# Attention over normalised feature maps: a prologue in units of 512 columns, f moved by DMA, and weighing begun ahead of the second chunk's scores

## The chip, the cores and the metric

The kernel runs on one core of a Trainium2 chip. The metric is the device time in microseconds (us) of one execution. The kernel before takes 1973.11 us, the median of 3 runs from 1971.37 to 1973.39.

Five engines work side by side, each through its own list of instructions in order, and wait for one another by semaphores: PE (TensorE, matrix products), DVE (VectorE), ACT (ScalarE), POOL (GpSimd) and SP (SyncE), which here issues all DMAs. An instruction that waits holds up everything behind it on its engine.

## The reference

For each of 4 images of 256 channels and 4096 pixels, what is computed is

```
n      = groupnorm(x)                 # 32 groups of 8 channels, over channels and pixels
f, g   = Wq n, Wk n                   # 64 x 4096 each
h      = Wv n                         # 256 x 4096
beta   = softmax(f^T g, axis=1)       # 4096 x 4096: over the rows, for each column m
out    = x + gamma * (h beta) + n     # 256 x 4096
```

## The kernel before

An image is a batch (b). Its 4096 output columns are done in 16 chunks of 256, so there are K = 64 chunks; k counts them through all images, and j is the chunk's number in its image. The 4096 rows of a chunk's scores are done in G = 8 groups of 4 x 128 rows. A step n = 8k + g is one group of one chunk. Every product is made of float16 parts, high and low (F1 holds f with high and low part in its two halves of partitions, G1 and GL hold g's high and low parts, V both parts of h).

The main loop goes over the 512 steps. At step n PE weighs: `weigh` multiplies the exponentials PH and PL of the step with V (24 matmuls of 256 or 257 columns). At each even step it first makes the scores of two groups (`scores(q)`, 16 matmuls into the two halves of S) of the chunk two ahead, q = n + 16. ACT copies each of these tiles to SBUF (`store`) and makes exponentials (`exps`, twice), DVE takes running maxima (`maximum`), turns and reduces them once a chunk (`turn_maxima`, `quadrant_maxima`, `column_maxima`, `spread_maxima`) and subtracts them (`subtract`), and POOL makes PL (`low_weights`). In the middle of a chunk PE sums maxima over partitions (`share_maxima`).

A finished chunk is scaled and turned by DVE (`turn_blocks`), regrouped by 16 small DMAs (`regroup`, 32 partitions each), added to the residual by POOL (`add_attention`) and stored (`store` on SP). SP's list for chunk k is: regroup(k-1), store(k-1), the residual's input for k+1, an input piece where one is due, and then the doubling of g.

Before the first step stands the prologue: image 0 is loaded in four pieces of 1024 columns, measured, normalised in place by DVE, split into XH (ACT) and XL (DVE for the first 128 channels, POOL for the others). PE waits for both parts of a piece, then projects f and g (`project_fg`, 8 units of 512 columns, in three banks of O); ACT and DVE split the result into F1, G1, GL by two instructions each over 64 partitions. Then come the scores of chunks 0 and 1 and 16 projections of h (`project_v`), and only then the first subtraction, exponential and weighing.

Units alternate which half of the partitions holds f (`halves`). scores needs g on both halves of the partitions, so SP copies g over (`double_g`). For the next image, the units of f and g are projected in chunk j = 13 (units 0 to 6, one a step) and the first step of j = 14 (unit 7), those of h in j = 15 and j = 0. The scores of the next image begin at the first step of j = 14.

There, the pair made at step g (even) reads f of units g and g+1. The lines before, by which each step can be followed, are L214 to L288 (SP), L303 to L349 (POOL), L436 to L506 (PE), L547 to L585 (ACT) and L767 to L868 (DVE).

Of the kernel before, what the change touches and what calls it, by code (L numbers as in the profile page):

```python
# [5 lines left out]
def groupnorm_attention(nc, x, wqT, wkT, wvT, gamma, out):  # L6
# [51 lines left out]
    NV = 2 * G  # L58
    assert len(FG_AT) == NFG and len(V_AT) + len(V_LATE) == NV
# [4 lines left out]
    with ExitStack() as ctx:  # L64
# [62 lines left out]
        gd2 = MB[:, M + 128:M + 128 + 32].rearrange("p (a b) -> p a b", a=NG)  # L127

        w_in = sem("w_in")
        x0_in = [sem(f"x0_in{i}") for i in range(NPC)]  # L130
# [11 lines left out]
        res_coefs = sem("res_coefs")  # L142
        xn_ready = sem("xn_ready")
# [4 lines left out]
        fg_done = sem("fg_done")  # L148
        g_in = [sem(f"g_in{i}") for i in range(NFG)]
# [35 lines left out]

        def halves(u):

            top, bottom = slice(0, CQ), slice(CQ, P)
            return (bottom, top) if u % 2 else (top, bottom)
# [25 lines left out]
        def _(sp):  # L215
            for q in range(NPC):
                sp.dma_start(x0[:, :, piece(q)], xv[0, :, :, piece(q)]).then_inc(x0_in[q], 16)
# [30 lines left out]

            def double_g(u):

                f, g = halves(u)
                n = slice(u % NFG * FGW, (u % NFG + 1) * FGW)
                sp.wait_ge(fg_done, u + 1)
                sp.dma_start(GG[f, :, n], GG[g, :, n]).then_inc(g_in[u % NFG], 16)

            residual_input(0)
            for u in range(NFG):
                double_g(u)
            for k in range(K):
                b, j = divmod(k, CPB)  # L260
                if k > 0:
                    regroup(k - 1)
                    store(k - 1)
# [3 lines left out]
                if b + 1 < BATCH:  # L267
                    p = j - STAT_FIRST + 1
                    if 0 <= p < NPC:
                        if p > 0:  # L270
                            sp.wait_ge(xin_read, b * NPC + p)
                        elif b > 0:
                            sp.wait_ge(xl_ready[1], NPC * (b + 1))
                            sp.wait_ge(xl_ready[0], NPC * (b + 1))
                        load(b + 1, p)
                    p = j - NORM_FIRST + 1
                    if j == STAT_FIRST + NPC - 1:
                        sp.wait_ge(xin_read, (b + 1) * NPC)
                        load(b + 1, 0)
                    elif 0 < p < NPC:  # L280
                        sp.wait_ge(xl_ready[1], NPC * (b + 1) + p)
# [9 lines left out]
        def _(pool):  # L291
# [11 lines left out]
            for q in range(NPC):  # L303
                pool.wait_ge(xh_ready, 2 * q + 2)
                pool.tensor_tensor(XL[:, 1, piece(q)], x0[:, 1, piece(q)], XH[:, 1, piece(q)],
                                   ALU.subtract).then_inc(xl_ready[1], 1)
# [24 lines left out]
            def low_input(b, p):  # L331
                for h in range(H):
                    pool.wait_ge(xh_ready, 2 * (NPC * b + p) + h + 1)
                    pool.tensor_tensor(XL[:, h, piece(p)], xin[:, h, :], XH[:, h, piece(p)],
                                       ALU.subtract).then_inc(xl_ready[h], 1)
# [16 lines left out]
        def _(pe):  # L352
            mm = nc.tensor.matmul

            def project_fg(u, o):

                b, i = divmod(u, NFG)
                for h in range(H):
                    pe.wait_ge(xl_ready[h], b * NPC + i // 2 + 1)
                n = slice(i * FGW, (i + 1) * FGW)  # L360
                w = slice(i % 2 * CQ, i % 2 * CQ + P)
                for h in range(H):
                    mm(o, wqkh[:, h, w], XH[:, h, n], start=h == 0, stop=False)
                    mm(o, wqkl[:, h, w], XH[:, h, n], start=False, stop=False)
                    m = mm(o, wqkh[:, h, w], XL[:, h, n], start=False, stop=h == H - 1)
# [72 lines left out]
            for i in range(NFG):  # L438
                if i >= OB:
                    pe.wait_ge(fg_done, i - OB + 1)  # L440
                project_fg(i, O[:, i % OB, :])
                if i % 2 == 1 and i >= 3:
                    pe.wait_ge(fg_done, i - 1)
                    if i == 3:
                        pe.wait_ge(g_in[0], 16)
                    scores((i // 2 - 1) * 2)
            pe.wait_ge(fg_done, NFG)
            scores(G - 2)
            for u in range(NV):
                if u >= 2:  # L450
                    pe.wait_ge(v_done, u - 1)
                project_v(u, O[:, u % 2, :])
                if u % 2 == 1 and u < G:
                    scores(G + u - 1)
                if u == 8:
                    share_maxima(0, O[:, 2, :])
# [14 lines left out]
            for n in range(K * G):  # L471
                k, g = divmod(n, G)
                b, j = divmod(k, CPB)
                if g % 2 == 0 and k + 2 < K:
                    nb, i = divmod(k + 2, CPB)
                    if i == 0:
                        pe.wait_ge(fg_done, nb * NFG + g + 2)
                    if g == 0 and i % 2 == 0:
                        pe.wait_ge(g_in[i // 2], 16 * (nb + 1))
                    if g == 4:  # L480
                        pe.wait_ge(mxc_ready, k + 2)
                    scores(n + 2 * G)
                pe.wait_ge(pl_ready, n + 1)
                if g == 0:
                    if k == 0:
                        pe.wait_ge(mxc_ready, 1)
# [10 lines left out]
                if g == 3 and k + 1 < K:  # L497
                    read = min(n + 2 * G + 1, K * G)
# [10 lines left out]
        def _(act):  # L509
# [16 lines left out]
            def round_fg(u, o):  # L526
                f, g = halves(u)
                n = slice(u % NFG * FGW, (u % NFG + 1) * FGW)
# [21 lines left out]
            for q in range(NPC):  # L550
                for h in range(H):
                    act.wait_ge(xn_ready, H * q + h + 1)
                    nc.scalar.copy(XH[:, h, piece(q)], x0[:, h, piece(q)]).then_inc(xh_ready, 1)
            for i in range(NFG):
                round_fg(i, O[:, i % OB, :])
                if i % 2 == 1 and i >= 3:
                    if i == 3:
                        for h in range(H):
                            act.wait_ge(xl_ready[h], NPC)
                    store(i - 3)  # L560
                    store(i - 2)
            store(G - 2)
            store(G - 1)
            for u in range(NV):
                round_v(u, O[:, u % 2, :])
                if u % 2 == 1 and u < G:
                    store(G + u - 1)
                    store(G + u)
            for s in range(EXP_LEAD):
                exps(s)  # L570

            for n in range(K * G):
# [4 lines left out]
                if g % 2 == 0 and k + 2 < K:  # L577
                    store(n + 2 * G)
                    store(n + 2 * G + 1)
                extra(k, g, MID)  # L580
                extra(k, g, END)
                if g in (4, 6) and b + 1 < BATCH and NORM_FIRST <= j < NORM_FIRST + NPC:
                    p, h = j - NORM_FIRST, g // 2 - 2
                    act.wait_ge(xn_ready, H * ((b + 1) * NPC + p) + h + 1)
# [3 lines left out]
        def _(dve):  # L588
# [128 lines left out]
            def low_fg(u, o):  # L717
                f, g = halves(u)
                n = slice(u % NFG * FGW, (u % NFG + 1) * FGW)
# [54 lines left out]
            for q in range(NPC):  # L774
                dve.wait_ge(x0_in[q], 16)
                for a in range(2 * q, 2 * q + 2):
                    for h in range(H):
                        last = ve.bn_stats(stats[:, h, a, :], x0[:, h, a * 512:(a + 1) * 512])
# [7 lines left out]
            for q in range(NPC + 1):  # L786
                if q < NPC:
                    for h in range(H):
                        normalise(x0[:, h, piece(q)], h).then_inc(xn_ready, 1)
                if q > 0:  # L790
                    dve.wait_ge(xh_ready, 2 * q)
                    ve.tensor_tensor(XL[:, 0, piece(q - 1)], x0[:, 0, piece(q - 1)], XH[:, 0, piece(q - 1)],
                                     ALU.subtract).then_inc(xl_ready[0], 1)
                if q == 0:
                    dve.wait_ge(w_hi, 1)
                    ve.tensor_tensor(wqkl[:, :, :], wqk[:, :, :], wqkh[:, :, :], ALU.subtract).then_inc(w_split, 1)
                    ve.tensor_tensor(wvl[:, :, :], wv[:, :, :], wvh[:, :, :], ALU.subtract).then_inc(w_split, 1)
            for i in range(NFG):
                low_fg(i, O[:, i % OB, :])
                if i % 2 == 1 and i >= 3:  # L800
                    maximum(i - 2)
                    maximum(i - 3)
            maximum(G - 1)
            maximum(G - 2)
            turn_maxima(0)
            for u in range(NV):
                low_v(u, O[:, u % 2, :])
                if u % 2 == 1 and u < G:
                    maximum(G + u)
                    maximum(G + u - 1)  # L810
                if u == 5:
                    quadrant_maxima(0)
                if u == G - 1:
                    turn_maxima(1)
                if u == 10:
                    column_maxima(0, O[:, 2, :])
                    spread_maxima(0)
# [77 lines left out]
```

## Time and profile before

| | |
|---|---|
| median of 3 runs | 1973.11 us |
| the profiled execution | 1974.76 us, its span 1973.0 us |
| mean granted TensorE clock | 0.993 of full speed |
| PE busy | 96% of the span |
| DVE, ACT, POOL busy | 82%, 81%, 66% |
| first matmul | 29.82 us |
| first weighing matmul | 104.88 us |

The engine table says how long each engine was busy. The timeline has an instruction (or several alike, merged, with their count) in each row: its start, how long it took, engine, line, operation, and in brackets how long the engine had been idle and what released it. The landing of a DMA is counted from its issue on SP. PEclk is the clock granted to TensorE as a share of full speed; 1.00 is its 2.4 GHz level and 0.50 its 1.2 GHz level.

### The profile page before, as it was taken

To read this page: it belongs to the slowest core of one execution; us is meant where nothing else is said; L and a number is where in the kernel's file an instruction comes from. 1 tells how busy PE (TensorE), PEld (TensorE's weight loads), DVE (VectorE), ACT (ScalarE), POOL (GpSimd) and SP (SyncE) were. 2 spreads that over 40 slices of the span, in tenths; PEclk is the share of its full clock that TensorE was granted. 3 is DMA by queue.
4 is the path that set the end of the run, shared out by engine and by line. 5 is a ranking of instruction groups with operands and counts; after the bars stand their busy time and mean duration, and the time that the engine had idled before them with its cause. 6 is when DMAs were issued, how large, how long until landed. Compare 5 with 4: busy or idle time off the path is not lost. (4 is left out here: it accounts for less than half of the span.)

```text
span 1973.0 us, 44069 instructions
## 1 busy us (share of the span) xinstructions
PE 1899.5 (96%) x17476; PEld 1565.3 (79%) x17476; DVE 1617.9 (82%) x1961; ACT 1590.3 (81%) x1699; POOL 1299.8 (66%) x746
## 2 busy tenths in 40 slices
PE   2889999999999999999999999999999999999999
PEld 1578888887788888888777888888878788888887
DVE  7778899888777899897876889998787778878784
ACT  3588888988777888898876888889887688888885
POOL 2066767876546766887554677688655476676776
PEclk9899999999999999999999999999999999999999
DMA  3012212211112121221110221121111011111111
GB/s 110 12 31 73 75 23 54 73 31 23 49 23 69 46 75 30 61 67 23 47 25 17 74 73 54 24 75 53 30 41 32 18 33 33 23 32 31 32 32 35
DMA packets 193629, 86.97 MB, mean 44 GB/s; under 512 B 149137, under 2 KB 186257, under 8 KB 193425
## 3 DMA queue, kind: packets, MB, share of 16 engines
q1 hardware_dynamic: 193424, 84.16, 16.2%
q8 instruction: 139, 2.28, 0.5%
q14 instruction: 66, 0.53, 0.1%
HBM read 46.60 MB, written 16.78 MB: 32 GB/s over the span
## 5 line engine op out<-in xcount | busy, mean ns | idle before, releaser
L310 POOL TENSOR_TENSOR PL<-SC,PH 128x1024 f16<-128x1024 f32 x512 | 1091.3, 2137 | 636.3 <-ACT SC L524 634.3
L416 PE MATMUL O<-V,PH 128*128 128x257 f16 x4096 | 1119.9, 273 | 9.4 <-POOL PL L310 5.2
L418 PE MATMUL O<-V,PL 128*128 128x257 f16 x4096 | 1119.8, 273 | 0.0
L417 PE MATMUL O<-V,PH 128*128 128x256 f16 x4096 | 1118.1, 273 | 0.0
L523 ACT ACTIVATE PH<-SC 128x1024 f16<-128x1024 f32 x512 | 540.6, 1056 | 134.3 <-PE O L418 121.6
L714 DVE TENSOR_TENSOR SC<-SC,MB 128x1024 f32<-128x1024 f32 x512 | 614.9, 1211 | 0.4
L517 ACT ACTIVATE SC<-S 128x1024 f32<-128x1024 f32 x512 | 502.5, 1012 | 124.5 <-issue 106.2
L674 DVE TENSOR_TENSOR XM<-S,XM 128x1024 f32<-128x1024 f32 x384 | 468.1, 1219 | 130.6 <-PE S L404 129.2
L524 ACT ACTIVATE SC<-SC 128x1024 f32<-128x1024 f32 x512 | 534.8, 1044 | 0.0
L416 PEld LDWEIGHTS O<-V,PH 128*128 128x128 f16 x4096 | 406.6, 99 | 59.2 <-DVE OSB L750 6.0
L417 PEld LDWEIGHTS O<-V,PH 128*128 128x128 f16 x4096 | 401.3, 98 | 50.7
L418 PEld LDWEIGHTS O<-V,PL 128*128 128x128 f16 x4096 | 401.4, 98 | 50.3
L398 PE MATMUL S<-GG,F 128*128 128x256 f16 x1024 | 155.5, 275 | 7.4 <-DVE XM L674 3.8
L401 PE MATMUL S<-GG,F 64*128 64x256 f16 x2048 | 158.0, 274 | 0.0
L404 PE MATMUL S<-GG,F 128*128 128x256 f16 x1024 | 157.8, 277 | 0.0
L669 DVE TENSOR_TENSOR XM<-S,SC 128x1024 f32<-128x1024 f32 x64 | 78.3, 1224 | 92.7 <-ACT SC L517 92.7
L404 PEld LDWEIGHTS S<-GG,F 128*128 128x128 f16 x1024 | 79.7, 98 | 61.1 <-issue 54.8
L401 PEld LDWEIGHTS S<-GG,F 64*128 64x128 f16 x2048 | 79.5, 95 | 60.9 <-issue 54.5
L398 PEld LDWEIGHTS S<-GG,F 128*128 128x128 f16 x1024 | 100.1, 98 | 24.7 <-issue 9.2
L728 DVE TENSOR_TENSOR V<-O,V 128x512 f16<-128x512 f32 x64 | 43.6, 688 | 62.0 <-ACT V L537 61.6
L537 ACT CAST V<-O 128x512 f16<-128x512 f32 x64 | 37.1, 587 | 66.6 <-PE O L377 66.6
L329 POOL TENSOR_TENSOR RES<-RES,ATT 128x512 f32<-128x512 f32 x63 | 80.6, 1280 | 0.9 <-DMA ATT<-OT 0.9
(84 smaller groups left out, 1138.5 us busy)
## 6 DMA issues: line engine op xcount, KB each, us to landing
xin<-x SPq DMA_DIRECT2D x24, 1024.0 KB, 5.9
xres<-x SPq DMA_DIRECT2D x64, 256.0 KB, 2.9
out<-RES SPq DMA_DIRECT2D x64, 256.0 KB, 2.2
ATT<-OT SPq DMA_DIRECT2D x1008, 16.0 KB, 1.9
SC<-x SPq DMA_DIRECT2D x4, 1024.0 KB, 8.7
GG<-GG SPq DMA_DIRECT2D x32, 128.0 KB, 2.4
SC<-wvT SPq DMA_DIRECT2D x1, 256.0 KB, 9.4
SC<-wqT SPq DMA_DIRECT2D x2, 64.0 KB, 10.5
```

The source lines that it names most:

```text
L310: pool.tensor_tensor(PL[:, s % RING, :], sc(s), PH[:, s % RING, :], ALU.subtract).then_inc(pl_ready, 1)
L398: mm(to(a, i), F1[:, rows(a, i)], G1[:, cols], start=True, stop=False)
L401: mm(to(a, i), F1[half, rows(a, i)], GL[half, cols], start=i % 2 == 1, stop=i % 2 == 0)
L404: m = mm(to(a, i), F1[:, rows(a, i)], G1[:, cols], start=False, stop=True)
L416: mm(o[:, 0:C + 1], PH[:, n % RING, cols], vh, start=t == 0, stop=False)
L417: mm(o[:, 0:C], PH[:, n % RING, cols], vl, start=False, stop=False)
L418: w = mm(o[:, 0:C + 1], PL[:, n % RING, cols], vh, start=False, stop=t == T - 1)
L517: nc.scalar.activation(sc(q), S[:, q % 2, :], ACT.Copy).then_inc(s_stored, 1)
L523: nc.scalar.activation(PH[:, s % RING, :], sc(s), ACT.Exp, bias=SHIFT)
L524: nc.scalar.activation(sc(s), sc(s), ACT.Exp, bias=SHIFT).then_inc(exp_done, 1)
L674: ve.tensor_tensor(XM[:, :], scores, XM[:, :], ALU.max).then_inc(s_maxed, 1)
L714: ve.tensor_tensor(tile, tile, MB[:, 0:M].unsqueeze(1).to_broadcast([P, GT, M]), ALU.subtract).then_inc(sub_ready, 1)
```

## The change

- The input of image 0 comes in eight pieces of 512 columns. Per unit, ACT makes XH straight from x with scale and bias, DVE normalises the first 128 channels into a spare bank of S (`x0n`), POOL the others into `xin` (`x1n`), and each subtracts XH to get its XL. The low parts of the weights move from DVE to POOL.
- PE begins a unit's products with XH before its XL is there, and projects h of a unit right behind its f and g, in five banks (three of O, two of S).
- The result of `project_fg` is rounded whole: one ACT instruction writes G1 and one DVE instruction GL, over all 128 partitions. f is then in G1 and GL, and two DMAs (`move_f`) take its parts to F1. `double_g` overwrites f's place with g and so waits until both have landed (semaphores `f_in`). scores waits for `f_in` of its two units where it had waited for `fg_done`. This holds for all four images.
- `SCORES_AT` says at which step which pair of score tiles is made. The prologue makes the pairs 0 to 6 (chunk 0) and 8 and 10; pairs 12 and 14 come in steps 1 and 2, chunk 2's in steps 4 to 7, one a step, and from step 8 on the order is the old one.

```diff
+    SCORES_AT = {1: 12, 2: 14, 4: 16, 5: 18, 6: 20, 7: 22}
+    SCORES_AT.update({n: n + 2 * G for n in range(G, (K - 2) * G, 2)})
...
+            def move_f(u):
+
+                f, g = halves(u)
+                sp.wait_ge(fg_done, u + 1)
+                sp.dma_start(F1[f, unit(u)], G1[f, unit(u)]).then_inc(f_in[u % NFG], 16)
+                sp.dma_start(F1[g, unit(u)], GL[f, unit(u)]).then_inc(f_in[u % NFG], 16)
+
             def double_g(u):
 
                 f, g = halves(u)
-                n = slice(u % NFG * FGW, (u % NFG + 1) * FGW)
-                sp.wait_ge(fg_done, u + 1)
-                sp.dma_start(GG[f, :, n], GG[g, :, n]).then_inc(g_in[u % NFG], 16)
+                sp.wait_ge(f_in[u % NFG], 32 * (u // NFG + 1))
+                sp.dma_start(GG[f, :, unit(u)], GG[g, :, unit(u)]).then_inc(g_in[u % NFG], 16)
...
                 if k > 0:
                     regroup(k - 1)
+                    if j == FG_FIRST + 1 and b + 1 < BATCH:
+                        move_f((b + 2) * NFG - 1)
+                        double_g((b + 2) * NFG - 1)
                     store(k - 1)
...
-                    for place, i in FG_AT.items():
-                        if place[0] == j:
-                            double_g((b + 1) * NFG + i)
+                    if j == FG_FIRST:
+                        for u in range((b + 1) * NFG, (b + 2) * NFG - 1):
+                            move_f(u)
+                            double_g(u)
...
             def project_fg(u, o):
...
                 for h in range(H):
-                    pe.wait_ge(xl_ready[h], b * NPC + i // 2 + 1)
...
+                    if b == 0:
+                        pe.wait_ge(xl_ready[h], i + 1)
+                    m = mm(o, wqkh[:, h, w], XL[:, h, unit(i)], start=False, stop=h == H - 1)
...
+            for u in range(NFG):
+                if u >= 3:
+                    pe.wait_ge(v_done, u - 2)
+                project_fg(u, first_bank(2 * u))
+                if u >= 2:
+                    pe.wait_ge(fg_done, u - 1)
+                project_v(u, first_bank(2 * u + 1))
...
+            for i in range(G // 2):
+                pe.wait_ge(f_in[2 * i], 32)
+                pe.wait_ge(f_in[2 * i + 1], 32)
+                if i == 0:
+                    pe.wait_ge(g_in[0], 16)
+                scores(2 * i)
+                later_v(NFG + 1 + i)
+            later_v(NFG + 5)
+            scores(G)
+            later_v(NFG + 6)
+            share_maxima(0, shared0)
+            later_v(NFG + 7)
+            scores(G + 2)
...
             def round_fg(u, o):
...
-                nc.scalar.copy(F1[f, n], o[f, :])
-                nc.scalar.copy(G1[g, n], o[g, :]).then_inc(fg_hi, 1)
+                nc.scalar.copy(G1[:, unit(u)], o).then_inc(fg_hi, 1)
...
             def low_fg(u, o):
...
-                ve.tensor_tensor(F1[g, n], o[f, :], F1[f, n], ALU.subtract)
-                ve.tensor_tensor(GL[g, n], o[g, :], G1[g, n], ALU.subtract).then_inc(fg_done, 1)
+                ve.tensor_tensor(GL[:, unit(u)], o, G1[:, unit(u)], ALU.subtract).then_inc(fg_done, 1)
```

Two places in the order of instructions matter. The first is SP's list in chunk 13, where the next image's units are handed over, and at the start of chunk 14. GG<-GG is a doubling of g, ATT<-OT the regrouping, xres<-x the residual's input. Before:

```order
L234 DMA out<-RES 128x2x256 [waits out_ready]
L226 DMA xres<-x 128x2x256 [waits res_ready]
L254 DMA GG<-GG 64x2x512 [waits fg_done] x7
L243 DMA ATT<-OT 32x4x32 [waits out_ready,osb_turned]
L243 DMA ATT<-OT 32x4x32 x15
L234 DMA out<-RES 128x2x256 [waits out_ready]
L226 DMA xres<-x 128x2x256 [waits res_ready]
L254 DMA GG<-GG 64x2x512 [waits fg_done]
```

Now, from the last of the seven units on (F<-GG are the two pieces of f; the six units before it have the same three rows with their own semaphore):

```order
L270 DMA F<-GG 64x512 [waits fg_done]
L271 DMA F<-GG 64x512
L277 DMA GG<-GG 64x2x512 [waits f_in6]
L260 DMA ATT<-OT 32x4x32 [waits out_ready,osb_turned]
L260 DMA ATT<-OT 32x4x32 x15
L270 DMA F<-GG 64x512 [waits fg_done]
L271 DMA F<-GG 64x512
L277 DMA GG<-GG 64x2x512 [waits f_in7]
L251 DMA out<-RES 128x2x256 [waits out_ready]
```

Seven doublings in a row have become seven groups of three DMAs, each with a wait for the landing of the two before it; unit 7 has moved ahead of the store of chunk 13's result, but still stands behind the regrouping.

The second place is DVE's list around the end of the prologue. V<-O is the low part of h, XM a maximum, SC<-SC,MB a subtraction. Before, between the second chunk's transposition of maxima and the first step:

```order
L680 STREAM_TRANSPOSE MT<-XM 128x1024
L728 TENSOR_TENSOR V<-O,V 128x2x256 x3
L700 TENSOR_REDUCE mxc<-O 128x8
L707 STREAM_TRANSPOSE MB<-mxc 128x256
L728 TENSOR_TENSOR V<-O,V 128x2x256 x5
L714 TENSOR_TENSOR SC<-SC,MB 128x1024 x4
L669 TENSOR_TENSOR XM<-S,SC 128x1024
```

Now, from the first chunk's transposition on:

```order
L745 STREAM_TRANSPOSE MT<-XM 128x1024
L750 TENSOR_REDUCE MB<-MT 128x8
L757 TENSOR_TENSOR mxs<-place,MB 128x32
L790 TENSOR_TENSOR V<-O,V 128x2x256 x2
L765 TENSOR_REDUCE mxc<-MB 128x8
L772 STREAM_TRANSPOSE MB<-mxc 128x256
L779 TENSOR_TENSOR SC<-SC,MB 128x1024
L734 TENSOR_TENSOR XM<-S,SC 128x1024
```

The first subtraction now stands ahead of the second chunk's first maximum, where before it stood behind all eight tiles of that chunk and all of h.

## Rows read from the trace of the kernel before

**Rows 1.** The page, engine table: busy us, share of the span, instructions.

```profile
PE 1899.5 (96%) x17476; PEld 1565.3 (79%) x17476; DVE 1617.9 (82%) x1961; ACT 1590.3 (81%) x1699; POOL 1299.8 (66%) x746
```

**Rows 2.** Timeline, DVE, start: start us, us, instruction [idle before <-releaser].

```profile
14.09 2.47 DVE L778 BATCH_NORM_STATS2 stats<-SC 128x6 f32<-128x512 f32 x4 [0.18 <-DMA SC<-x]
22.50 0.15 DVE L650 SCALAR_TENSOR_TENSOR rbias<-nmean,nrstd 128x2 f32<-128x2 f32 x1
```

**Rows 3.** Groups by form: busy us, mean ns | idle before.

```profile
L319 POOL TENSOR_SCALAR RES<-xres,rscale,rbias 128x256 f32<-128x256 f32 x128 | 70.4, 561 | 0.0
L721 DVE TENSOR_TENSOR F<-O,F 64x512 f16<-64x512 f32 x32 | 22.1, 689 | 24.6 <-ACT GG L531 24.3
L530 ACT CAST F<-O 64x512 f16<-64x512 f32 x32 | 18.5, 580 | 15.2 <-PE O L365 15.2
```

**Rows 4.** Timeline, normalisation of image 0 on DVE and POOL.

```profile
33.88 3.34 DVE L654 TENSOR_SCALAR SC<-SC,nmean,nrstd 128x1024 f32<-128x1024 f32 x2
33.98 2.69 POOL L305 TENSOR_TENSOR XL<-SC,XH 128x1024 f16<-128x1024 f32 x1 [1.70 <-ACT XH L553]
```

**Rows 5.** Timeline, ACT, two projections of h in a row.

```profile
91.06 0.59 ACT L537 CAST V<-O 128x512 f16<-128x512 f32 x1 [2.71 <-PE O L377]
92.37 0.59 ACT L537 CAST V<-O 128x512 f16<-128x512 f32 x1 [0.72 <-PE O L377]
```

**Rows 6.** Timeline, PE and DVE, a pair of score tiles in the prologue.

```profile
78.27 0.61 PE L398 MATMUL S<-GG,F 128*128 128x256 f16 x4 [0.19 <-DVE XM L674]
...
80.00 2.58 DVE L674 TENSOR_TENSOR XM<-S,XM 128x1024 f32<-128x1024 f32 x2 [0.23 <-PE S L404]
...
82.64 0.61 PE L398 MATMUL S<-GG,F 128*128 128x256 f16 x4
```

**Rows 7.** Timeline, the first weighing, and the scores of step 8.

```profile
100.61 1.06 ACT L523 ACTIVATE PH<-SC 128x1024 f16<-128x1024 f32 x1 [1.88 <-DVE SC L714]
...
102.69 8.40 POOL L310 TENSOR_TENSOR PL<-SC,PH 128x1024 f16<-128x1024 f32 x4 [61.17 <-ACT SC L524]
...
104.88 0.40 PE L416 MATMUL O<-V,PH 128*128 128x257 f16 x1 [5.25 <-POOL PL L310]
...
133.13 0.60 PE L398 MATMUL S<-GG,F 128*128 128x256 f16 x4
```

**Rows 8.** Windows, PE after the wait that ended at 104.88: stretch, its length, PE busy, PEclk, DMA share, GB/s.

```profile
106.00:108.00 2.00, 2.00 (x11) 0.50 0.00 0
```

**Rows 9.** Timeline, SP, the three handovers to the next image.

```profile
495.97 5.24 SPq L254 DMA_DIRECT2D GG<-GG  x7
511.93 10.31 SPq L243 DMA_DIRECT2D ATT<-OT  x16
...
974.59 5.24 SPq L254 DMA_DIRECT2D GG<-GG  x7
...
1453.87 5.22 SPq L254 DMA_DIRECT2D GG<-GG  x7
```

**Rows 10.** Timeline, PE, the same stretches.

```profile
500.42 0.60 PE L398 MATMUL S<-GG,F 128*128 128x256 f16 x4
...
516.73 0.38 PE L425 MATMUL S<-mxs,alike 128*128 128x32 f32 x2 [2.09 <-issue]
...
526.63 0.60 PE L398 MATMUL S<-GG,F 128*128 128x256 f16 x4
...
1005.58 0.60 PE L398 MATMUL S<-GG,F 128*128 128x256 f16 x4
...
1483.28 0.60 PE L398 MATMUL S<-GG,F 128*128 128x256 f16 x4
```

**Rows 11.** One line's DMAs: the doubling of g (L254), then the regrouping (L243).

```profile
L254 SPq DMA_DIRECT2D GG<-GG x32: 590/608/981, 41.0 to 1487.3; - x32
DMA to landing us min/median/max: 2.3/2.4/4.2
...
DMA to landing us min/median/max: 1.8/1.9/3.6
```

More of the change, by code:

```diff
@@ L148, in groupnorm_attention @@
         fg_done = sem("fg_done")
+        f_in = [sem(f"f_in{i}") for i in range(NFG)]
         g_in = [sem(f"g_in{i}") for i in range(NFG)]
@@ L215, in _ @@
         def _(sp):
-            for q in range(NPC):
-                sp.dma_start(x0[:, :, piece(q)], xv[0, :, :, piece(q)]).then_inc(x0_in[q], 16)
+            for u in range(NFG):
+                sp.dma_start(x0[:, :, unit(u)], xv[0, :, :, unit(u)]).then_inc(x0_in[u], 16)
             sp.dma_start(wqk[:, :, 0:CQ], wqT.rearrange("(h p) q -> p h q", p=P)).then_inc(w_in, 16)
@@ L549, in _, with later_v @@
             nc.scalar.copy(wvh[:, :, :], wv[:, :, :]).then_inc(w_hi, 1)
[L550 to L569, printed above, removed]
+            act.wait_ge(res_coefs, 1)
+            for u in range(NFG + 2):
+                if u < NFG:
+                    for h in range(H):
+                        nc.scalar.activation(XH[:, h, unit(u)], x0[:, h, unit(u)], ACT.Identity,
+                                             bias=rbias[:, 0, h:h + 1], scale=nrstd[:, h:h + 1]).then_inc(xh_ready, 1)
+                if u >= 2:
+                    round_fg(u - 2, first_bank(2 * (u - 2)))
+                    round_v(u - 2, first_bank(2 * (u - 2) + 1))
+            def later_v(u):
+                round_v(u, O[:, u % OB, :])
+            later_v(NFG)
+            act.wait_ge(w_split, 2)
+            for i in range(G // 2):
+                store(2 * i)
+                store(2 * i + 1)
+                later_v(NFG + 1 + i)
+            later_v(NFG + 5)
+            for h in range(H):
+                act.wait_ge(xl_ready[h], NFG)
+            store(G)
+            store(G + 1)
+            later_v(NFG + 6)
+            later_v(NFG + 7)
+            exps(0)
+            store(G + 2)
+            store(G + 3)
+            for s in range(1, EXP_LEAD):
                 exps(s)
@@ L576, in _ @@
                     exps(n + EXP_LEAD)
-                if g % 2 == 0 and k + 2 < K:
-                    store(n + 2 * G)
-                    store(n + 2 * G + 1)
+                q = SCORES_AT.get(n)
+                if q is not None:
+                    store(q)
+                    store(q + 1)
                 extra(k, g, MID)
@@ L773, in _ @@
             ve.memset(cv[:, :], 1.0)
[L774 to L778, printed above, removed]
+            for u in range(NFG):
+                dve.wait_ge(x0_in[u], 16)
+                for h in range(H):
+                    last = ve.bn_stats(stats[:, h, u, :], x0[:, h, unit(u)])
             last.then_inc(x0_measured, 1)
@@ L798, in _ @@
[L798 to L804, printed above, removed]
-            turn_maxima(0)
[L806 to L817, printed above, removed]
@@ L818, in _, with first_half @@
-            for s in range(SUB_LEAD):
+            def first_half(u):
+                if u >= 2:
+                    dve.wait_ge(xl_ready[0], u - 1)
+                ve.tensor_scalar(x0n[:, u % 2, :], x0[:, 0, unit(u)], nmean[:, 0:1], nrstd[:, 0:1],
+                                 ALU.subtract, ALU.mult).then_inc(x0n_ready, 1)
+            first_half(0)
+            for u in range(NFG + 2):
+                if u < NFG:
+                    if u + 1 < NFG:
+                        first_half(u + 1)
+                    dve.wait_ge(x0n_ready, u + 1)
+                    dve.wait_ge(xh_ready, H * u + 1)
+                    ve.tensor_tensor(XL[:, 0, unit(u)], x0n[:, u % 2, :], XH[:, 0, unit(u)],
+                                     ALU.subtract).then_inc(xl_ready[0], 1)
+                if u >= 2:
+                    low_fg(u - 2, first_bank(2 * (u - 2)))
+                    low_v(u - 2, first_bank(2 * (u - 2) + 1))
@@ new lines, in later_v @@
+            def later_v(u):
+                low_v(u, O[:, u % OB, :])
+            later_v(NFG)
+            for i in range(G // 2):
+                maximum(2 * i + 1)
+                maximum(2 * i)
+                if i < G // 2 - 1:
+                    later_v(NFG + 1 + i)
+            turn_maxima(0)
+            quadrant_maxima(0)
+            later_v(NFG + 4)
+            later_v(NFG + 5)
+            column_maxima(0, shared0)
+            spread_maxima(0)
+            subtract(0)
+            maximum(G + 1)
@@ L819, in _ @@
+            maximum(G)
+            later_v(NFG + 6)
+            subtract(1)
+            later_v(NFG + 7)
+            maximum(G + 3)
+            maximum(G + 2)
+            for s in range(2, SUB_LEAD):
                 subtract(s)
@@ L826, in _ @@
                     scale_output(k - 1)
-                if g % 2 == 0 and k + 2 < K:
-                    maximum(n + 2 * G + 1)
+                q = SCORES_AT.get(n)
+                if q is not None:
+                    maximum(q + 1)
                 if n + SUB_LEAD < K * G:
                     subtract(n + SUB_LEAD)
-                if g % 2 == 0 and k + 2 < K:
-                    maximum(n + 2 * G)
+                if q is not None:
+                    maximum(q)
+                if n == 2:
+                    turn_maxima(1)
+                    quadrant_maxima(1)
                 if g == 7 and k + 2 < K:
```

123 lines of the change are left out of this document (62 added, 61 removed).

## The prediction

> **What bounds the kernel now.** I read the engine table first: PE is busy for 96% of the span [rows 1]. So time is to be had only where PE stands still or runs at its lower clock. PE's timeline says where that is: it does no weighing before 104.88 [rows 7], and in the main loop it waits little, the longest of it at the three places where one image hands over to the next (2.09 us before a sum of maxima at 516.73, a little more at the other two) [rows 10]. The change touches both places, so I worked each out: the time at which PE begins the scores of step 8, 133.13 before [rows 7], from which on the order is the old one, and the handovers, where f now goes by DMA.
>
> **The prologue: coefficients.** The last four measurements of x wait for the last piece at 14.09 and take 2.47, 0.62 each [rows 2]. With pieces half as large two remain, so the coefficients, ready at 22.65, are ready at 21.4. The bounds are no gain and 1.6.
>
> **The prologue: units.** ACT makes two XH of 512 columns (0.58 each, the time of a copy of 64x512 [rows 3]), so PE starts at about 22.7. A projection of h takes PE 1.31, the distance of two roundings [rows 5]; f and g of a unit have the same number of columns, so a unit takes 2.6. Eight units and the ninth h make 22.2. The first 3 us after a wait run at half the clock (0.50 in 106 to 108 [rows 8]), which costs 1.5. PE is through at 46.3. Is another engine later? DVE has four instructions a unit. At 0.69 [rows 3] they are 2.8, eight units 22.1 from 21.5 on, so it ends beside PE. POOL has two: a tensor_scalar of twice 0.56 [rows 3] and a subtraction of half of 2.1, the time of 128x1024 [rows 7], together 2.2. Beside DVE's in-place normalisation such a subtraction took 2.69 and DVE's pair 3.34 [rows 4]. With these the two are 2.5 to 2.9 a unit. I take 2.4, hidden behind PE; 2.9 would put the scores 2 us later.
>
> On this last point a rule of the Trainium skill bears: "VectorE: DVE Perf Modes", section "Why PSUM operands drop a tier", says that the double-rate mode of fp32 needs both SBUF read ports and isn't to be had with a PSUM operand. DVE's new target is in PSUM, so by the rule its slow-down beside POOL [rows 4] should not come back, and POOL would stay near 2.2 a unit. The trace of before has no such instruction. By either the sum is the same, since 2.2 and 2.5 both hide behind 2.6.
>
> **The prologue: scores.** From the start of a pair to DVE's first maximum are 1.73, the two maxima take 2.58 less an overlap, and the next pair starts behind them [rows 6]. Before, with two projections of h between, the pairs stood 4.37 apart [rows 6]; with one between, PE has 2.9 of work and the chain of 4.2 sets the distance. Four pairs end at 46.3 + 17.2 = 63.5. Then DVE turns, reduces, takes two low parts, spreads and subtracts: the subtraction ends at 69.6. ACT has a store that waits for the next maximum (70.7) and two roundings ahead of the first exponential, so that starts at 72.9. Exponential to POOL is 2.1, POOL to weighing 2.2 [rows 7]: weighing begins at 77.1, 27.8 earlier.
>
> **The ramp.** Most of that is given back. Steps 0 to 7 now hold six pairs of tiles instead of four. A weighing has twice the columns of a projection of h, 2.62 [rows 5], a pair takes PE 1.52 (the 1.73 of [rows 6] less the way to DVE). The 8 weighings are 21.0, six pairs 9.1, the sum of maxima 0.4. To this come 3.1 for two starts at half the clock (step 0, and behind the wait in step 3), and waits: 1.9 for the maxima ahead of pair 14, 2.5 for the maxima of chunk 1, which DVE turns only after pair 14, and 1.1 ahead of most pairs from step 5 to step 8, because a pair and a weighing (4.1) are shorter than the way of a pair through DVE (1.73, then a maximum, a subtraction and a maximum, 1.15 each: 5.2): 4.7 in all. The sum is 42.7, so step 8 starts at 119.8 instead of 133.13: **13.3 less**. Bounds: 5 less, if POOL needs 2.9 a unit and each of the chains in the ramp is a third longer; 18 less, if the waits of the ramp but one fall away.
>
> **The handovers.** Here the change adds waits to SP's list. Before, SP issued the seven doublings in one go, from T = 495.97, 974.59 and 1453.87, in 5.2 us, and the regrouping came 16 us after T and took 10.31 [rows 9]. Now each unit is two moves and one doubling that waits for the second move's landing, and behind this wait stand the next unit's moves, then the regrouping, then unit 7. An issue takes 0.61, 0.64 with the gap [rows 11]. A landing: 2.4 for the doubling's 128 KB, 1.9 for the regrouping's 16 KB [rows 11]; a move has 64 KB, I take 2.3. One unit is 0.64 + 2.3 + 0.64 = 3.58, seven are 25.1. The regrouping, ready at T + 16, is held until T + 25.1 and ends at T + 35.4. Unit 7's second move is issued at T + 36.0 and lands at T + 38.3. T itself comes 0.6 earlier, since ACT's list in this chunk is one rounding of 0.58 a step shorter [rows 3]: T + 37.7 on the old scale.
>
> PE needs unit 7 for the pair of step 6 of chunk 14. Before it started that pair at 526.63, 1005.58 and 1483.28 [rows 10], T + 30.7, T + 31.0 and T + 29.4. So it starts 7.0, 6.7 and 8.3 later, 22.0 in all. Whatever PE gains ahead of that pair, such as the 2.09 of row 516.73 (DVE and ACT have an instruction less for each unit), is swallowed by this wait, and so is a new one of about 1.5 at the chunk's first step, where units 0 and 1 are due at T + 4.45 (500.42 [rows 10]) and unit 1 lands at T + 5.9. After 10 us of idleness PE runs at half the clock for 3 us, as at 104.88 [rows 8]: 1.5 each, 4.5. POOL's addition waits for the regrouping as well, but PE stands still until later. **26.5 more** in all. Bounds by landings of 1.9 and 2.5: seven units change by 2.8 less and 1.4 more, the last move by 0.4 and 0.2, so 17 and 31.5.
>
> A rule of the skill gives the same thing another price: "DMA: Bandwidth & Descriptors", section "Anatomy of one DMA", has 2.0 us fixed plus bytes at 436 GB/s (measured on GpSimd's path) and says that a wait is made by the issuing sequencer before dispatch. For 64 KB that is 2.15, an estimate from the page; the trace's 1.9 and 2.4 lie on both sides. With 2.15 the handovers would cost 3.6 less in all.
>
> **The sum.** 1974.76, the profiled execution, less 13.3 plus 26.5 is 1988. The median of the runs is 1.65 below the profiled execution, so I predict 1986.
>
> **Rivals.**
> 1. *The moves of f are hidden, faster.* If SP did not stand at its wait but let the queue hold the doubling, seven units would be issued in 21 x 0.64 = 13.4, the regrouping would start at T + 16 as before, and unit 7 would land at T + 26.3 + 2.9 = T + 29.2, just where PE comes. The three waits before the sum of maxima would go too (about 7 with 3 for the half clock). 1973 - 13 - 10 = 1950. It decides from a unit cost of 2.3 us or less. For it: DVE and ACT do get shorter lists. Against it: SP's list is in order, and before, the same seven doublings took 5.24 rather than 4.5, since SP stood for the last unit [rows 9]. 10%.
> 2. *The prologue gives nothing, slower.* POOL at 2.9 a unit and beyond, PE falling to half the clock in every gap between the pairs, and the chains of the ramp longer by a third: 3 gained, 1996. For it: the trace's 2.69 and 3.34 [rows 4]. Against it: DVE no longer works in place, and the pairs before kept 4.37 at full clock. 15%.
> 3. *The ramp runs smoothly.* If DVE and ACT work off the six pairs with one short wait, the gain is 18 to 20, and with landings of 2.0 the handovers cost 18: 1973. 15%.
>
> The forecast has 60%. The range of 8 in 10 is 1972 to 1997: it takes in rival 3 and rival 2 and leaves out rival 1. A difference of 0.2%, 4 us, is what a measurement of this kernel can tell from none. Faster than that: rival 1 and a little of rival 3, 0.12. Within it: 0.08, from rival 3. Slower: 0.80.
>
> **What would show it.** In the profile after, PE's wait list should name the moves of f (F<-GG) or "issue" before the scores line, three times 8 to 11 us, in step 6 of chunk 14, and three times 1 to 2 in its first step. SP's rows should show seven groups 3.6 apart from T on, the regrouping starting 25 after T, and the moves of unit 7 behind it. The waits before the sums of maxima at the handovers should be gone. The first weighing should stand at 77 and the scores of step 8 at 120. The forecast is wrong if the seven groups take less than 18 us, if PE's wait in chunk 14 is under 4 us, or if step 8 starts before 113 or after 128.

## The result and the profile after

The changed kernel takes 1996.4 us, the median of 4 runs from 1992.83 to 1999.40. The kernel before took 1973.25 us beside it (4 runs, 1971.37 to 1973.46). The ratio is 1.0119, its 95% interval 1.0096 to 1.0141: slower. The forecast was 1986, from 1972 to 1997. The execution that was profiled is the longest of the four, 1999.40 us with a span of 1997.6, so I compare it with the profiled 1974.76 and keep in mind that it lies 3 us above the median. The median lies in the range, only 0.6 us below its upper end.

The page of the changed kernel, engine table and one row of the DMA issues (KB each, us to landing):

```profile
PE 1904.3 (95%) x17476; PEld 1568.2 (79%) x17476; DVE 1591.1 (80%) x1931; ACT 1574.7 (79%) x1675; POOL 1315.6 (66%) x760
...
F<-GG SPq DMA_DIRECT2D x64, 64.0 KB, 2.0
```

DVE and ACT have less to do than in [rows 1], 27 and 16 us, and PE is busy 5 us more with the same instructions. So the time was lost in waits. PE's list of waits (total us, times, longest) says where it came from:

```profile
PE S L442 <- issue: 27.7, 3, 10.0
...
PE S L442 <- DMA F<-GG: 6.9, 3, 3.3
```

Both rows are the handovers. "issue" is a wait whose releaser the profile doesn't show, three times close to 10 us. The timeline of PE shows their places (start, us, ..., [idle before <-releaser]), and what became of the sum of maxima and the first weighing:

```profile
49.48 0.39 PE L409 MATMUL S<-XL,wqkh 128*128 128x512 f16 x1 [0.52 <-POOL XL L344]
...
52.32 0.60 PE L442 MATMUL S<-GG,F 128*128 128x256 f16 x4
...
84.35 0.40 PE L460 MATMUL O<-V,PH 128*128 128x257 f16 x1 [2.46 <-POOL PL L349]
...
127.17 0.61 PE L442 MATMUL S<-GG,F 128*128 128x256 f16 x4 [0.95 <-DVE XM L739]
...
494.96 0.60 PE L442 MATMUL S<-GG,F 128*128 128x256 f16 x4 [1.19 <-DMA F<-GG]
...
526.61 1.01 PE L442 MATMUL S<-GG,F 128*128 128x256 f16 x4 [9.55 <-issue]
...
1016.26 1.01 PE L442 MATMUL S<-GG,F 128*128 128x256 f16 x4 [10.03 <-issue]
...
1505.66 1.01 PE L442 MATMUL S<-GG,F 128*128 128x256 f16 x4 [8.08 <-issue]
```

Against [rows 7] the first weighing is 20.5 us earlier, but the scores of step 8 (127.17) only 6.0. Against [rows 10] the pair of step 6 follows a wait of 8 to 10 us, and no wait over 0.2 us is left before a sum of maxima in the handovers. SP's timeline of the first handover shows what PE waits for:

```profile
488.70 0.53 SPq L270 DMA_DIRECT2D F<-GG  x1
489.28 0.60 SPq L271 DMA_DIRECT2D F<-GG  x1
491.54 0.63 SPq L277 DMA_DIRECT2D GG<-GG  x1
492.22 0.61 SPq L270 DMA_DIRECT2D F<-GG  x1
492.87 0.60 SPq L271 DMA_DIRECT2D F<-GG  x1
494.89 0.62 SPq L277 DMA_DIRECT2D GG<-GG  x1
...
512.53 0.62 SPq L277 DMA_DIRECT2D GG<-GG  x1
513.25 10.33 SPq L260 DMA_DIRECT2D ATT<-OT  x16
523.63 0.60 SPq L270 DMA_DIRECT2D F<-GG  x1
524.56 0.51 SPq L271 DMA_DIRECT2D F<-GG  x1
526.53 0.63 SPq L277 DMA_DIRECT2D GG<-GG  x1
```

Behind the second move, issued at 489.28, SP stands until it has landed and issues the doubling only at 491.54, and so in every group. Most groups are 3.3 to 3.4 us apart (doublings at 491.54 and 494.89), a few 4.2 to 5.6. The regrouping begins 24.6 us after T = 488.70 (before, 16 after [rows 9]), in the other two handovers 26.5 and 27.1 after, and unit 7's second move is issued behind all 16 of its DMAs, at 524.56. PE's pair starts 2.05 later, at 526.61: one landing.

The difference of the profiled spans is 24.6. To place it I follow three marks of both timelines, the first projection of h behind each handover: 577.08, 1056.34 and 1533.74 before, 579.97, 1068.86 and 1557.63 after, so the changed kernel is 2.9, 12.5 and 23.9 late there. It was 6.0 early at step 8. On this scale the three handovers cost 8.9, 9.6 and 11.4, together 29.9, and the rest of the kernel 0.7: 30.6 - 6.0 = 24.6.

### The profile page after: what moved, and what is told of

Its sections match the earlier page's. It is cut to its first block and busy times, and to the rows that moved or that the text cites. A ratio compares the mean times of both kernels' runs of the same rounds, so it can differ in the third digit from the quotient of the medians.

```text
span 1997.6 us, 44149 instructions
## 1 busy us (share of the span) xinstructions
PE 1904.3 (95%) x17476; PEld 1568.2 (79%) x17476; DVE 1591.1 (80%) x1931; ACT 1574.7 (79%) x1675; POOL 1315.6 (66%) x760
## 5 line engine op out<-in xcount | busy, mean ns | idle before, releaser
L442 PE MATMUL S<-GG,F 128*128 128x256 f16 x1024 | 155.8, 275 | 46.1 <-issue 27.7
```

What stands on the lines that cost most here:

```text
L442: mm(to(a, i), F1[:, rows(a, i)], G1[:, cols], start=True, stop=False)
```

## The experiments

All changes are to the changed kernel unless it is said otherwise. In each experiment one number is from the runs (the median) and the rest from one profiled execution. Step 8 varies between executions whose prologue is the same: 127.17 in the changed kernel, 123.96 in E1 and 126.08 in E2. E1 to E4 share nine runs of the kernel before (1971.47 us), E5 and E6 seven (1971.29 us).

### E1: the doubling one unit behind its moves

```diff
                         for u in range((b + 1) * NFG, (b + 2) * NFG - 1):
                             move_f(u)
-                            double_g(u)
+                            if u > (b + 1) * NFG:
+                                double_g(u - 1)
+                        double_g((b + 2) * NFG - 2)
```

> The changed kernel with one edit at the handovers: the doubling of unit u-1 is issued behind the moves of unit u, as the prologue does it, so SP does not stand for a landing at each unit. Unit 7 stays behind the regrouping. Theory A (SP stands at the wait for each landing, which holds back the regrouping and unit 7): the seven units take 21 issues of 0.64 and one wait, about 15 us instead of 24.5; the regrouping starts 16 after the first move, unit 7 lands at 29 after it; PE's waits of 9.55, 10.03 and 8.08 shrink to under 2 each, most of the half clock behind them goes, and the time is 1960 to 1968. Rival B (the moves themselves, as traffic or by their landing, hold up PE wherever they stand): the waits stay above 6 and the time is within 5 of 1996.

1965.03 us (1963.41 to 1965.65), 0.9959 of the kernel before, interval 0.9944 to 0.9974. SP's timeline in the first handover:

```profile
489.12 0.60 SPq L270 DMA_DIRECT2D F<-GG  x1
489.76 0.60 SPq L271 DMA_DIRECT2D F<-GG  x1
490.40 0.62 SPq L277 DMA_DIRECT2D GG<-GG  x1
491.06 0.60 SPq L270 DMA_DIRECT2D F<-GG  x1
...
501.65 10.31 SPq L260 DMA_DIRECT2D ATT<-OT  x16
512.01 0.60 SPq L270 DMA_DIRECT2D F<-GG  x1
512.95 0.52 SPq L271 DMA_DIRECT2D F<-GG  x1
```

A unit now costs 1.94 (489.12 to 491.06), three issues and no landing. The regrouping begins 16.2 us after the first move (485.46), as in the kernel before, and PE's waits at step 6 shrink:

```profile
515.26 0.60 PE L444 MATMUL S<-GG,F 128*128 128x256 f16 x4 [2.19 <-issue]
```

The other two are 1.22 and 0.58. The same DMAs in another order are worth 31.4 us, so the cost was SP's standing still, not the transfers. By the profiles the spans differ by 34.9 (1997.6 to 1962.7). Of this 3.2 are there at step 8 already (123.96 instead of 127.17), where the edit changes nothing. The other 31.7 agree with the medians: 23.7 in the waits at step 6, 2.9 in those of the first step (6.9 to 4.0), and some 5.5 in the half clock behind the waits of step 6, which cost 7.1 in the changed kernel (below) and here 1.6, only at the first handover: 32.1 in all. Theory A held; only the wait of 2.19 is a little over its "under 2".

### E2: unit 7's moves ahead of the regrouping

```diff
                 if k > 0:
-                    regroup(k - 1)
                     if j == FG_FIRST + 1 and b + 1 < BATCH:
                         move_f((b + 2) * NFG - 1)
+                    regroup(k - 1)
+                    if j == FG_FIRST + 1 and b + 1 < BATCH:
                         double_g((b + 2) * NFG - 1)
```

> The changed kernel with one edit at the handovers: the two moves of unit 7 stand ahead of the regrouping; the waits for each landing stay. Theory A: the seven units still take 24.5, unit 7 lands at 27 after the first move, before PE comes to it, so the waits of 8 to 10 before the scores of step 6 go; the regrouping still starts 10 late, POOL's addition with it, and the low weights behind it may cost PE 1 to 3 in the next chunk. Time 1965 to 1975. Rival C (the late regrouping, through POOL, is what holds PE, and unit 7 is late only beside it): PE's wait moves to the weighing and stays at 6 or more each, time above 1985.

1966.07 us (1964.14 to 1968.80), 0.9970, interval 0.9958 to 0.9982. Here the groups keep their landings (490.69 to 494.03 from doubling to doubling), yet PE has no wait at step 6 at all. SP and then POOL and PE, first handover:

```profile
512.81 0.60 SPq L270 DMA_DIRECT2D F<-GG  x1
513.46 0.60 SPq L271 DMA_DIRECT2D F<-GG  x1
514.17 11.65 SPq L260 DMA_DIRECT2D ATT<-OT  x16
...
527.46 1.27 POOL L369 TENSOR_TENSOR RES<-RES,ATT 128x512 f32<-128x512 f32 x1 [9.58 <-DMA ATT<-OT]
...
530.86 0.28 PE L461 MATMUL O<-V,PH 128*128 128x257 f16 x1 [2.41 <-POOL PL L350]
```

So the path needs both of its parts: slow groups and the regrouping ahead of unit 7. Taking either away gives the time back. The late regrouping then comes out on POOL, which stands for it 9.58, 6.37 and 7.01 us at the three handovers. Only at the first does it hand anything on to PE, 2.41. Theory A held here too. Rival C, by which the late regrouping is a cost of its own, fell in size: 2.41 us, once.

### E3: POOL multiplies and adds

```diff
-            pool.wait_ge(coefs_ready, 1)
+            pool.wait_ge(res_coefs, 1)
...
-                pool.tensor_scalar(x1n[:, u % 2, :], x0[:, 1, unit(u)], nmean[:, 1:2], nrstd[:, 1:2],
-                                   ALU.subtract, ALU.mult).then_inc(x1n_ready, 1)
+                pool.tensor_scalar(x1n[:, u % 2, :], x0[:, 1, unit(u)], nrstd[:, 1:2], rbias[:, 0, 1:2],
+                                   ALU.mult, ALU.add).then_inc(x1n_ready, 1)
```

> The changed kernel with one edit in the prologue: POOL normalises by multiply and add (scale, and bias = -mean x scale) instead of subtract and multiply, on the same 128x512 tile. In the trace the second takes 2078 ns, while multiply and add on 128x256 takes 557. Theory D (the pair of operations decides): the instruction falls to 1.1 us, POOL's unit from 3.3 to 2.4, the first scores start at 46.5 to 48 instead of 52.3, and the time falls by 4 to 6. Rival E (the width or the target tile decides): it stays at 2.0 or more and the time at 1996.

The changed kernel's POOL, groups by form (busy us, mean ns | idle before):

```profile
L340 POOL TENSOR_SCALAR xin<-SC,nmean,nrstd 128x512 f32<-128x512 f32 x8 | 16.6, 2078 | 2.9 <-DVE nrstd L712 2.9
```

E3's, and PE at the start of its scores and at step 8:

```profile
L340 POOL TENSOR_SCALAR xin<-SC,nrstd,rbias 128x512 f32<-128x512 f32 x8 | 6.2, 772 | 3.1 <-DVE rbias L715 3.1
...
48.87 0.60 PE L442 MATMUL S<-GG,F 128*128 128x256 f16 x4
...
121.61 0.61 PE L442 MATMUL S<-GG,F 128*128 128x256 f16 x4 [0.95 <-DVE XM L739]
```

The same values in the same shape cost 2078 ns as a subtraction and a multiplication and 772 ns as a multiplication and an addition. Theory D held on the instruction, and by more than it said. The 2078 don't come from DVE working beside it: they are 2.07 to 2.12 whether DVE normalises at that moment or not (2.08 at 46.11, when DVE does none).

The first scores come at 48.87, later than the 46.5 to 48 expected. Counted from rbias (ready at 22.25 against 23.15) they take 26.6 us, where the changed kernel, E1 and E2 take 29.1 to 29.2. So the edit is worth 2.5 us there, and 3.1 in E5 and E6, where it is 26.1. PE's waits for POOL's XL are gone, which cost 3.9 in the changed kernel (below), but PE's half rate at the start lasts longer. Step 8 is 5.6 us earlier than in the changed kernel, but only 2.4 earlier than in E1; what is over the 2.5 isn't shown to be the edit's. The kernel took 1992.03 us (1990.94 to 1993.09), 1.0097, interval 1.0082 to 1.0112: 4.4 less than the changed kernel (whose fastest run, 1992.83, lies in this spread) and as much less than E4, still slower than the one before, since its waits at step 6 are the same (27.5 in all).

### E4: five pieces instead of eight

```diff
-            for u in range(NFG):
+            for q in range(NPC - 1):
+                sp.dma_start(x0[:, :, piece(q)], xv[0, :, :, piece(q)]).then_inc(x0_in[2 * q], 16)
+            for u in range(NFG - 2, NFG):
                 sp.dma_start(x0[:, :, unit(u)], xv[0, :, :, unit(u)]).then_inc(x0_in[u], 16)
```

> The changed kernel with one edit: image 0 is loaded in three pieces of 1024 columns and two of 512 instead of eight of 512. In the changed kernel the last piece landed at 15.34, before at 14.09. Theory F (issuing eight DMAs of x takes SP 4.9 us instead of 2.3, and the small pieces stretch the load): the last piece lands at 14.1 to 14.5, rbias is ready at 21.5 to 22.2 instead of 23.15, and the time falls by 1 to 1.5. Rival G (the landing is set by the bytes, and what came later is chance): the last piece lands at 15 or later and nothing changes.

1996.47 us (1995.40 to 1997.37), 1.0119, interval 1.0102 to 1.0136: no gain. With a late first piece the statistics run back to back and set the end themselves:

```profile
6.10 9.96 DVE L841 BATCH_NORM_STATS2 stats<-SC 128x6 f32<-128x512 f32 x16 [4.58 <-DMA SC<-x]
```

They end at 16.06, those of the changed kernel at 16.63, so 0.6 us is all there was. Step 8 came at 125.55, 1.6 earlier than in the changed kernel but between those of E1 and E2, and the median didn't move. Theory F's gain of 1 to 1.5 did not come. The last piece of the eight lands at 15.34, 14.14 and 14.33 in the changed kernel, E1 and E3, which have the same transfers. The coefficient term can't be told apart from this chance.

### E5: the edits of E1, E2 and E3 together

> The changed kernel with the three edits together: doublings issued one unit behind the moves, unit 7's moves ahead of the regrouping, POOL's normalisation by multiply and add. If the three losses are what they were measured to be apart (handovers 30 of which each edit alone gave back about the same 30; POOL 5.6), the sum holds: with unit 7 early the remaining waits of e1 at step 6 (2.19, 1.22, 0.58) go as well, scores of step 8 start at 121.6, and the time is 1955 to 1960. Rival: with POOL's load of the prologue lightened another engine takes the unit stage over and the handover edits overlap in full; the time is 1961 to 1965.

1954.34 us (1953.79 to 1956.69), 0.9915, interval 0.9900 to 0.9929: faster than the kernel before by 17 us and than the changed one by 42, and just under the 1955 to 1960 expected. The handovers' 30 and POOL's few us add up; the rival's 1961 to 1965 is out. PE's waits at the handovers are the three of the first step alone, 0.62, 1.82 and this one:

```profile
1440.90 0.60 PE L445 MATMUL S<-GG,F 128*128 128x256 f16 x4 [2.36 <-issue]
```

Step 8 starts at 121.32, 11.8 before that of [rows 7]. The profiled span is 18.1 shorter (1954.9), so some 6 come from the rest. At the three marks of the handovers (560.92, 1036.85, 1514.91) E5 is 16.2, 19.5 and 18.8 early: the first two handovers gain 4.4 and 3.3, the third loses 0.7, and what is behind it another 0.7. The waits of 2.1 to 2.4 before the sums of maxima [rows 10] are gone, and 4.8 in the first steps have come, 2.36 of them at the third.

### E6: E5 with the weighing begun late

Pairs 12 and 14 and the maxima of chunk 1 are made in the prologue again, and chunk 2's pairs at the even steps.

```diff
-    SCORES_AT = {1: 12, 2: 14, 4: 16, 5: 18, 6: 20, 7: 22}
-    SCORES_AT.update({n: n + 2 * G for n in range(G, (K - 2) * G, 2)})
+    SCORES_AT = {n: n + 2 * G for n in range(0, (K - 2) * G, 2)}
...
             scores(G + 2)
+            scores(G + 4)
+            scores(G + 6)
```

> As e5_three, and the pairs 12 and 14 of chunk 1 are made in the prologue, with chunk 2's pairs back at the even steps 0, 2, 4, 6, so weighing is not begun ahead of the second chunk's scores. Theory H (the early weighing is given back in the ramp: steps 0 to 7 took 42.8 from first weighing to the scores of step 8, against 28.2 before, for two more pairs that cost 4.2 to 4.6 each where nothing else runs): weighing starts 9 later than in e5_three, at 89, and the scores of step 8 at 117 to 119, 3 to 4 earlier than in e5_three; time 3 to 4 less. Rival I (the early weighing gains, since it fills PE while the pairs pass through DVE and ACT): the scores of step 8 start at 124 to 129 and the time is 3 to 8 more than e5_three's.

1954.14 us (1952.52 to 1956.93), 0.9909, interval 0.9892 to 0.9925: the same as E5. The two ramps side by side, first E5 (the first weighing and step 8):

```profile
80.18 0.40 PE L463 MATMUL O<-V,PH 128*128 128x257 f16 x1 [3.52 <-POOL PL L352]
...
121.32 0.61 PE L445 MATMUL S<-GG,F 128*128 128x256 f16 x4 [0.95 <-DVE XM L742]
```

Then E6 (the last pairs of the prologue, the first weighing and step 8):

```profile
80.84 1.03 PE L444 MATMUL S<-GG,F 128*128 128x256 f16 x4 [3.83 <-DVE XM L747]
...
86.49 1.04 PE L444 MATMUL S<-GG,F 128*128 128x256 f16 x4 [2.68 <-DVE XM L747]
...
92.18 1.01 PE L444 MATMUL S<-GG,F 128*128 128x256 f16 x4 [2.72 <-DVE XM L747]
94.92 0.42 PE L462 MATMUL O<-V,PH 128*128 128x257 f16 x1
...
121.79 0.60 PE L444 MATMUL S<-GG,F 128*128 128x256 f16 x4
```

Begun 14.7 us earlier, E5's ramp takes 41.1 for steps 0 to 7, E6's 26.9, and step 8 differs by 0.5. Neither theory had that: one expected E6 to be 3 to 4 us faster than E5, the other 3 to 8 slower. What is shown is that moving the weighing ahead is worth nothing here. PE's windows in E6 (stretch, length, PE busy, PEclk, DMA share, GB/s):

```profile
80.00:86.00 6.00, 2.97 (x16) 0.50 0.01 3
```

So two readings remain, and no run parts them. By the first the chain of DVE and ACT bounds both orders, and in E5 the weighings merely fill PE's gaps. By the second E6's order is the better one and loses it again to the clock. E6's PE stood at 1.2 GHz from about 77 to 97 (PEclk 0.52 in 76 to 97), E5's only in the 3 us behind its first weighing. A pair stands in its own chain: PE has to finish it before DVE can start, and the next one waits 2.7 for DVE. At the half clock the pairs are 5.65 apart, at full clock they were 4.37 [rows 6]. Three such pairs are some 4 us, an estimate from these rows and about what theory H, with its 117 to 119, was off by.

## Why the prediction was right, and where it was off

**The handovers, right in mechanism, nearly in size.** Predicted 26.5 more, measured 29.9. Most groups were 3.34 apart instead of 3.58 and most landings 2.0 instead of 2.3, the regrouping began T + 24.6, 26.5 and 27.1 instead of T + 25.1, and PE's pair came at T + 37.9, 39.7 and 40.2 against T + 38.3. In the second and third handover some moves took up to 4.3 us to land, which ate more than the shorter landings gave. With the marks taken off, PE's pair of step 6 was 5.9, 7.8 and 9.9 later than before, 23.6 in all against the 22.0 forecast: about half of the miss of 3.4. The other half lies behind the pair. There the term that was too small is the half clock: I had 1.5 a handover, and behind the three waits it cost 3.1, 2.3 and 1.7, 7.1 instead of 4.5, of which 0.8 came back elsewhere. PE's windows there:

```profile
526.00:528.00 2.00, 1.39 (x10) 0.50 0.13 30
...
530.00:532.00 2.00, 2.00 (x11) 0.50 0.43 138
532.00:534.00 2.00, 2.00 (x16) 0.80 0.00 0
```

The matmuls of the long kind (0.42) end at 532.78, 6.2 us after 526.61, which costs 3.1. At the second the level lasts 4.7 us, at the third 3.3. I know no reason for the difference. The new waits in the first step were 1.19, 2.45 and 3.31, foreseen as 1.5, the last of them with a half clock of its own behind it; the waits before the sums of maxima went, as foreseen.

**The prologue, right in sign, half in size.** Predicted 13.3 less, measured 6.0. The step that failed is "POOL has two: a tensor_scalar of twice 0.56". I had priced subtract-and-multiply by a row of multiply-and-add [rows 3], as if the operations' names did not matter. It takes 2.07, a unit of POOL 3.30 (39.52 to 42.81, the starts of two such instructions), and PE, which needs 2.6, waits for POOL's XL from the third unit on. The two products with XL then start 0.67 to 0.68 further apart than without a wait (0.50 at the third unit): 3.9 in all. Coefficients ready at 23.15 instead of 21.4 are 1.7 more, and PE's first product 1.7 behind them instead of 1.3 is 0.4 (two XH take ACT 1.52, not 1.16). The half rate behind PE's first wait came as forecast, 1.4 instead of 1.5. That makes the 6.0 that the first scores (52.32) are behind the forecast (46.3). This half rate is in the matmuls' own rows, 0.43 apart at first and 0.22 from 27.7 on:

```profile
25.66 0.63 PE L404 MATMUL O<-XH,wqkh 128*128 128x512 f16 x1
26.09 0.63 PE L405 MATMUL O<-XH,wqkl 128*128 128x512 f16 x1
...
29.02 0.38 PE L405 MATMUL O<-XH,wqkl 128*128 128x512 f16 x1
29.24 0.38 PE L404 MATMUL O<-XH,wqkh 128*128 128x512 f16 x1
```

The windows show a granted clock of 1.00 from 20 to 50, so here they don't tell it. E3 confirms the first term: with it gone PE has no wait for XL, and the stage from the coefficients to the first scores is 2.5 shorter, the 3.9 less 1.4, since in E3 the half rate lasted 5.6 us (to about 29.6) instead of 2.8. The forecast had the ceiling of 2.9 a unit from a contention that POOL did not meet, and missed a cost that had nothing to do with it. The 6.0 at step 8 are also those of one execution: E1, with the same prologue, was 9.2 early there, E2 7.1.

On that contention the rule weighed in the prediction held for POOL, and DVE paid for it. POOL's subtraction of 512 columns takes 1.16 beside DVE's normalisation (25.20) and 1.15 without it (48.27), where [rows 4] have 2.69 for 1024. DVE's normalisation in place had taken 0.77 for 1024 columns while POOL stood idle, and 1.67 beside POOL [rows 4]:

```profile
22.58 1.53 DVE L654 TENSOR_SCALAR SC<-SC,nmean,nrstd 128x1024 f32<-128x1024 f32 x2
```

With its target in PSUM it takes 0.81 for 512 columns, whether POOL works or not: it always has the slow one of the two rates. "VectorE: DVE Perf Modes" of the Trainium skill, section "Why PSUM operands drop a tier", says this much, that an fp32 instruction with a PSUM operand doesn't get the double rate, and the trace agrees with 0.81. That POOL is left alone for the same reason is my reading.

**The pairs and the ramp, right.** From the first scores to the first weighing 32.0, predicted 30.8; from there to step 8 42.8, predicted 42.7 (41.1 in E1, E3 and E5). That most of the 28 us earlier start would be given back was foreseen; E5 and E6 make it stronger: what the weighing itself gains by standing ahead is given back whole.

**The coefficients, wrong by chance and a little more.** 21.4 was predicted, 23.15 came in the profiled execution and 22.1 to 22.7 in the others with eight pieces, since the last piece lands anywhere from 14.1 to 15.3. From the last measurement to rbias it took 0.4 longer than before, in the others up to 0.6, and that I didn't resolve.

**The sum.** 26.5 and 13.3 gave +13, the profile +24.6, the medians +23. The misses all point the same way and add up: 3.4 at the handovers, 7.3 in the prologue, and 0.7. The forecast was right in direction and mechanism, but its time of 1986 was 10 short, and that 1996.4 still lies in the range, like step 8's 127.17 under its bound of 128, is in part luck. Of the rivals, the second (prologue worth 3, 1996) came nearest in time. POOL did go beyond its 2.9 a unit, to 3.3, but by another mechanism than the one named, and its 1996 had the handovers at the forecast 26.5; the first fell, because SP does stand at its wait. The third's smooth ramp did not come either: 42.8, with a wait of 0.95 still ahead of step 8.

Open: why POOL's operation pair matters by a factor of 2.7, what stretches a landing to 4.3, how the half clock's length behind a wait comes about, why the granted clock of a window and the matmuls' own rate differ at PE's start, and why the changed kernel's runs spread from 1993 to 1999 while those of the kernel before keep within 2. The spread goes with the clock: the two long runs had a mean granted clock of 0.987, the two short ones 0.990 and 0.991.

## What to carry over

A wait for a DMA's landing on an in-order issuing queue is paid by everything queued behind it: price a list as issues plus landings, put the dependent DMA one unit behind, and look for what an urgent one is queued behind. Price an instruction by a row with the same pair of operations, engine and shape, and where there is none let the bound reach above the nearest. Starting an engine's work earlier need not bring the end point forward: here 14.7 us at the start were worth 0.5 at step 8, so compare both orders at the point from which they are alike.

## What the runs showed of the hardware

- POOL, 128x512 of fp32 with two per-partition scalars: subtract and multiply 2078 ns, multiply and add 772 ns.
- SP issues a DMA in 0.60 to 0.64 us. Two moves of 64 KB and a doubling that waits for them take 3.34 a unit in most cases, up to 5.6, and 1.94 when the doubling is one unit behind.
- A 64 KB move inside SBUF lands 2.0 us after its issue, in the worst case 4.3.
- After a wait of 8 to 10 us TensorE stood at its 1.2 GHz level for 3.3 to 6.2 us of work. At PE's first matmuls their spacing shows the half rate for 2.8 us (5.6 in E3) while the windows give a granted clock of 1.00.
- DVE, fp32 TENSOR_SCALAR: in place in SBUF 1024 columns take 0.77 us alone and 1.67 beside POOL; with the target in PSUM 512 columns take 0.81 with or without POOL, and POOL is not slowed.
